# A residual added by VectorE in PSUM instead of by GpSimd, and another order of a scan layer's work on four engines

## The reference

```
h = x @ fc1_w.T + fc1_b
xz = h @ in_proj_w.T;  xc, z = split(xz)
u = silu(conv4(xc) + conv_b)                     # 512 channels
dt_low, Bm, Cm = split(u @ x_proj_w.T)           # 16, 16, 16
dt = softplus(dt_low @ dt_proj_w.T + dt_proj_b)
h[t] = exp(dt[t] * A) * h[t-1] + dt[t] * u[t] * Bm[t];   y[t] = sum_n h[t] * Cm[t]   # 16 states
s = ((y + u * D) * silu(z)) @ out_proj_w.T @ fc2_w.T + fc2_b
g = (silu(xn @ wg.T) * (xn @ wu.T)) @ wd.T       # 768 hidden
out = x + s * silu(g)
```

## Time and profile before

| | us |
|---|---|
| median of 3 runs (3019.51 to 3027.25) | 3020.09 |
| the profiled execution | 3014.55 |
| its span | 3012.9 |
| the scan layer in it, from its first instruction | about 1010 to 3013 |

### The profile page before, as it was taken

The page is one execution under the profiler, slowest core; times in us unless marked ns, Lnnn a source line. Parts: engine busy times, 40 slices in busy tenths (PEclk is TensorE's granted clock), DMA queues, the critical chain, the costliest instruction groups (busy, mean ns, idle before and its releaser), DMA issues.

```text
span 3012.9 us, 43961 instructions
## 1 busy us (share of the span) xinstructions
PE 2588.0 (86%) x13290; PEld 1488.0 (49%) x13290; DVE 2306.4 (77%) x2777; ACT 2027.6 (67%) x3268; POOL 2069.9 (69%) x650
## 2 busy tenths in 40 slices
PE   6776188888887769998999899999899899999987
PEld 2333033333333435564665555656556566566455
DVE  6577466556562269989889799898798888989995
ACT  3221146656564379878788698797787887978874
POOL 0454430000000179999999899999899999999996
PEclk9998579989998879999999999999999999999999
DMA  8335497767641123032132130321312303213210
GB/s 274 105 103 127 109 266 210 186 175 180 172 140 46 55 120 120 30 119 100 36 120 85 65 120 33 117 99 36 121 52 97 120 17 126 105 38 120 78 63 7
DMA packets 133934, 323.21 MB, mean 107 GB/s; under 512 B 13233, under 2 KB 89009, under 8 KB 117314
## 3 DMA queue, kind: packets, MB, share of 16 engines
q1 hardware_dynamic: 113186, 248.84, 26.7%
q0 software_dynamic: 19200, 70.73, 7.1%
q10 hardware_dynamic: 1312, 0.66, 0.1%
HBM read 277.12 MB, written 43.13 MB: 106 GB/s over the span
## 4 chain that ended last, share of the span: by engine, by line
PE 26%; issue 12%; POOL 12%; ACT 7%; DVE 7%; ACTq 1%; DVEq 1%; DMA 0%; POOLq 0%; SPq 0%
PE l_p_w L1995 11%; PE l_p_y L1987 6%; POOL l_st L1638 5%; PE l_p_w L2041 5%; DVE l_st L1457 4%; POOL l_st L1630 3%; PE l_p_w L2060 3%; ACT l_p_a L1716 2%; POOL keep_xg L1638 2%; DVE keep_xg L1457 1%; ACT L1791 1%; POOL l_dtu L1644 1%; ACT L1725 1%; DVE keep_xg L1466 1%; PE l_p_w L2017 1%
## 5 line engine op out<-in xcount | busy, mean ns | idle before, releaser
L1457 DVE TENSOR_TENSOR_SCAN l_st<-l_p_a,l_hl,l_st 128x512 f32<-128x512 f32 x768 | 931.6, 1265 | 112.1 <-ACT l_p_a L1716 93.0
L1638 POOL TENSOR_TENSOR l_st<-l_st,l_cs 128x2048 f32<-128x2048 f32 x192 | 868.6, 4541 | 4.1 <-ACT l_hl L1721 3.8
L1716 ACT ACTIVATE l_p_a<-l_dt,lw_a_neg 128x512 f32<-128x512 f32 x1024 | 666.1, 681 | 51.6 <-DVE keep_xg L1457 40.4
L1630 POOL TENSOR_TENSOR l_st<-l_bs,l_dtu 128x2048 f32<-128x2048 f32 x128 | 580.9, 4539 | 47.5 <-PE l_p_y L1987 44.2
L1987 PEld LDWEIGHTS l_p_y<-keep_ident,l_st 128*128 128x128 f32 x3072 | 353.8, 144 | 136.9 <-POOL l_st L1638 74.8
L1987 PE MATMUL l_p_y<-keep_ident,l_st 128*128 128x128 f32 x3072 | 382.4, 281 | 42.9 <-POOL l_st L1638 42.9
L977 ACT ACTIVATE a_pr<-a_p_s 128x512 f32<-128x512 f32 x512 | 284.8, 596 | 163.9 <-PE a_p_s L1043 145.7
L901 DVE TENSOR_REDUCE a_mpart<-a_p_m 128x1 f32<-128x512 f32 x512 | 315.2, 683 | 98.2 <-PE a_p_m L1008 96.5
L1457 DVE TENSOR_TENSOR_SCAN keep_xg<-l_p_a,l_hl,keep_xg 128x512 f32<-128x512 f32 x256 | 314.8, 1267 | 2.3 <-DVE keep_xg L1466 1.9
L1638 POOL TENSOR_TENSOR keep_xg<-keep_xg,l_cs 128x2048 f32<-128x2048 f32 x64 | 290.7, 4542 | 11.0 <-ACT l_hl L1721 11.0
L1043 PE MATMUL a_p_s<-a_qst,kx 99*128 99x256 bf16 x1024 | 206.7, 292 | 73.6 <-ACT a_pr L977 54.8
(11 more groups left out here) (225 smaller groups left out, 3920.1 us busy)
## 6 DMA issues: line engine op xcount, KB each, us to landing
a_w<-in_w_dram POOLq DMA_DIRECT2D x64, 1024.0 KB, 12.0
l_bs<-s_bc SPq DMA_DIRECT2D x64, 1024.0 KB, 4.7
l_cs<-s_bc SPq DMA_DIRECT2D x64, 1024.0 KB, 4.9
keep_share<-s_x SPq DMA_DIRECT2D x32, 512.0 KB, 4.4
s_kp<-t_kp SPq DMA_DIRECT2D x96, 128.0 KB
kx<-s_kp SPq DMA_DIRECT2D x16, 768.0 KB, 11.8
s_vp<-t_vo SPq DMA_DIRECT2D x16, 544.0 KB
a_vg<-s_vp SPq DMA_DIRECT2D x16, 544.0 KB, 11.7
```

The costliest lines, as they stand in the source:

```text
L1457: eng.tensor_tensor_scan(st[k % NG][:, n, :], p_a[:, n, :], st[k % NG][:, n, :], hl[:, k, n:n + 1], ALU.mult, ALU.add).then_inc(scan_ok, 1)
L1630: eng.tensor_tensor(st[n][:, :, :], bs[:, 4 * n:4 * n + 4, :], dtu[(k // NG) % 2][:, :].unsqueeze(1).broadcast_to([P, NG, TT]), ALU.mult). ...
L1638: eng.tensor_tensor(st[n][:, :, :], st[n][:, :, :], cs[:, 4 * n:4 * n + 4, :], ALU.mult).then_inc(cm_ok, 1)
L1716: eng.activation(p_a[:, n, :], dt[c % 2][:, :], ACT.Exp, scale=a_neg[:, c, m:m + 1]).then_inc(dA_ok, 1)
```

## The change

`mixed` now does all of a tile's end: the product with the gate is written back into PSUM (`mixed_out`), and a third VectorE instruction adds `xt` and writes `gate`. GpSimd's `residual` and its semaphore `res_ok` are gone, and SyncE waits for the second half of `op` instead. Beside this the calls in `period` of all four engines stand in another order, and so does `FILLS`. The shape and number of the other operations are the same; GpSimd's stream only moves its period's start (weighed 11 and 12 now open the next period), does weighed(0) before step_input(1), and does the norm's small product earlier. The start of a tile's own exp rows, and gate_h(4), gate_h(5), gate_z(3), have moved over the border of the period, so that they are called for tile f.

```diff
-        FILLS = (("up", 4, END, 1), ("dt", 1, SCAN, 0), ("up", 5, END, 1), ("tr", 0, FRONT, 1), ("dn", 0, END, 0),
+        FILLS = (("yb", 2, END, 0), ("g", 4, END, 0), ("up", 4, END, 1), ("g", 5, END, 0), ("z", 3, END, 1),
...
@@ sync
-                        eng.wait_ge(res_ok, f + 1)
+                        taken(eng, "op", f, 1)
...
@@ vector, mixed
-                    eng.wait_ge(ob_ok, t * 2 + h + 1)
+                    eng.wait_ge(ob_ok, t * 4 + 2 * h + 1)
                     taken(eng, "dn", t, h)
-                    eng.tensor_tensor(gate[:, 2 * h:2 * h + 2, :], mixed_out, gate[:, 2 * h:2 * h + 2, :], ALU.mult)\
+                    eng.tensor_tensor(mixed_out, mixed_out, gate[:, 2 * h:2 * h + 2, :], ALU.mult).then_inc(ob_ok, 1)
+                    eng.wait_ge(ob_ok, t * 4 + 2 * h + 2)
+                    eng.wait_ge(old_in, t * 16 + 16)
+                    eng.tensor_tensor(gate[:, 2 * h:2 * h + 2, :], mixed_out, xt[:, 2 * h:2 * h + 2, :], ALU.add)\
                        .then_inc(done["op"], 1)
...
@@ gpsimd
-                def residual(t):
-                    taken(eng, "op", t, 1)
-                    eng.wait_ge(old_in, t * 16 + 16)
-                    eng.tensor_tensor(gate[:, :, :], gate[:, :, :], xt[:, :, :], ALU.add).then_inc(res_ok, 1)
...
@@ tensor, period, from up(4) on
                     if end:
+                        back(q, f, p, 2)
+                        sums(f, 12)
+                        gate_h(q, f, p, 4)
+                        sums(f, 13)
                         up_h(q, f, p, 4)
+                        gate_h(q, f, p, 5)
+                        gate_z(q, f, p, 3)
+                        up_h(q, f, p, 5)
...
```

More of the change, by code:

```diff
@@ L1511, in period @@
                         dbu(s, 0)
-                    if end:
-                        hidden(f, 3)
-                    if scan:
                         scan_unit(s, 0, 0)
+                        scan_unit(s, 0, 1)
                     if end:
@@ L1594, in period @@
                         scan_unit(s, 11, 3)
+                        gated(s, o, 1)
                         dbu(s, 12)
-                        hidden(s, 1)
+                    if nxt:
+                        norm_aggr(q + 1)
+                    if scan:
                         scan_unit(s, 12, 0)
@@ L1657, in period @@
                     if end:
+                        weighed(f, 11)
+                        weighed(f, 12)
                         dbu(f, 15)
@@ L1678, in period @@
                         step_input(s, o, 2)
-                    if end:
-                        residual(f)
-                    if scan:
                         weighed(s, 4)
@@ L1806, in period @@
                     if scan:
+                        exp_unit(s, 0, 0)
+                        exp_unit(s, 0, 1)
+                        exp_unit(s, 0, 2)
+                    if end:
+                        gate_h(f, 4)
+                    if scan:
+                        exp_tables()
                         exp_unit(s, 0, 3)
-                    if front:
-                        normed(q)
-                    if scan:
                         exp_unit(s, 1, 0)
@@ L2075, in period @@
                     if end:
+                        sums(f, 14)
+                        sums(f, 15)
                         down(q, f, 0)
+                        down(q, f, 1)
                     if front:
@@ L2079, in period @@
                     if end:
-                        sums(f, 15)
-                    if front:
-                        conv_in(q, q, p, 0)
-                        conv_in(q, q, p, 1)
-                    if end:
-                        down(q, f, 1)
                         back(q, f, p, 3)
@@ L2088, in period @@
                         sums(s, 0)
+                        gate_z(q, s, o, 0)
+                        gate_z(q, s, o, 1)
+                    if front:
+                        conv_in(q, q, p, 0)
+                    if scan:
+                        sums(s, 1)
+                        step_low(q, s, 2)
                     if end:
@@ L2111, in period @@
                         back(q, s, o, 0)
-                    if front:
-                        conv_in(q, q, p, 3)
-                    if scan:
-                        sums(s, 5)
-                        step_low(q, s, 3)
-                        sums(s, 6)
+                        up_h(q, s, o, 0)
+                        sums(s, 7)
+                        gate_h(q, s, o, 1)
+                        sums(s, 8)
+                        gate_h(q, s, o, 2)
+                        back(q, s, o, 1)
                     if front:
```

320 lines of the change are left out of this document (148 added, 172 removed).

## The result

The changed kernel takes 3056.75 us (median of 4 runs, 3056.18 to 3058.35), the kernel before 3023.67 beside it (3019.51 to 3027.87). The ratio is 1.011, with a 95% interval of 1.0091 to 1.0129: it is slower, by about 33 us. The forecast was 3049 with a range of 2998 to 3074. The profiled execution of the changed kernel took 3056.6 (span 3054.7), against 3014.55 before.

A forecast was written before the change was run, and what follows sets the result against it. The period was taken as GpSimd's own work plus waits for TensorE. Terms +35.4 (loop), +6.4 (outside), -10 (back edges), -3 (start) made +28.8 on 3014.55, 3043.4; with 5.5 to the median, 3049 us, range 2998 to 3074.

The forecast's parts named there:

- the two stretches: Weighed(15) to dbu(5), then dbu(5) to dbu(7): GpSimd would wait 5.0 us and 2.9 us for TensorE.
- the twelve periods: Loop periods without back-edge cost: each 121.0 us against 118.05, +2.95, adding +35.4 us over twelve.
- TensorE's three gaps: New TensorE waits before back(3), xc(0) and g(0): 0.45, 0.55 and 0.9 us per period in the loop.
- No other on GpSimd inside a period: GpSimd would wait inside a period only at dbu(5) and dbu(7), about 5 and 2.9 us, both released by TensorE.
- Outside the loop: Periods 14 and 15 would take 120.25 us each, +3.2 twice, +6.4 in all.
- the 0.55 of z(0): In the loop xc(0) waits 0.55 us for z(0)'s gate to load its table and read the bank.
- X: Stretch from weighed(15) to dbu(5): 24.2 us of TensorE's path in the loop, about 21.5 in period 16.
- The back edges: Loop jumps, now between up(3) and back(2): 2 us less per edge, -10 in all, bounds 0 and -29.
- Start and end: Period 1's weighed(0) no longer behind step_input(1): -3 us, bounds 0 and -4.5; the very end: 0.
- the clock rival: TensorE's clock drops between weighed(15) and dbu(7) each period: +27 us on top, 3076; chance 0.10.
- Edges hidden: Stops at the loop's jumps wholly hidden, waits at their floor: -16 us, 3004; chance 0.12.
- GpSimd's cut is the gain: GpSimd is the bound; waits stay 2.62, each of fifteen removed residuals saves 2.33 us: -35, 2985; chance 0.12.

## Why the prediction was right, and where not

**The waits.** Right in sign, place and size. The forecast for the two stretches was 5.0 and 2.9, measured 4.96 and 2.94; the period 121.0, measured 121.03; the twelve periods +35.4, measured +35.8. That they agree to a few hundredths is in part luck: TensorE's three gaps came to 1.50 and not 1.90, and the rest of its way through both stretches to about 0.7 more than I had added up. Leaving out 2.6 inside the first stretch shortened the period by 2.6, leaving out 1.7 inside the second by 1.0 to 1.7, and the same 1.7 outside them by nothing. The gaps were 0.34, 0.44 and 0.72 (forecast 0.45, 0.55, 0.9).

**"No other on GpSimd inside a period"** was wrong. Two of the four waits are put on GpSimd by ScalarE. It changed no number: the run with last(2) and last(4) early turned them into TensorE's.

**Outside the loop** I let the 0.55 of z(0) fall away, because the table would be loaded ahead. It did not. ScalarE itself was busy until 2810.0, so the load began when it does in the loop, and xc(0) waited 0.47:

```profile
2810.06 1.28 ACT L1778 ACT_TABLE_LOAD   x1
2811.35 1.27 ACT L1778 ACTIVATE l_sz<-l_p_w,lw_b_in 128x512 f32<-128x512 f32 x2
```

```profile
2812.18 1.96 PE L1985 MATMUL l_p_w<-l_xnT,lw_w_in 128*128 128x512 f32 x4 [0.47 <-ACT l_sz L1778]
```

The first period came to +3.8, not +3.2. The second is +4.7. I had said that without front blocks X would be 21.5, 2.3 of waiting; measured were 2.12 at weighed(2) and 1.87 at dbu(5), 4.0. Some of the +4.7 is the kernel before's: its period 15 to 16 took 115.02 in one profile and 116.75 in another with the same code there.

**The back edges** are the step where the path was wrong. I took 2 off each, -10, as TensorE had blocks from the jump to sums(15) to cover its stop. But GpSimd meets TensorE earlier, at dbu(1), which waits for sums(13). Ahead of that stand only back(2), sums(12) and g(4) behind the jump, and dbu(1) waits 1.71 to 3.81. The rest are waits for ScalarE's last(k), above all last(2), longer than in an undisturbed period. So each edge still costs 5.2 to 5.6. How long TensorE stands says little about that: where it stood 3.25 and not 4.48, its last block before the jump, up(3), had started later (76.7 after dbu(5), against 74.9), and it resumed at nearly the same time (81.9 and 81.4).

How much the edges gave back is not settled to better than some us. The two profiled executions say 3.3, the medians say more. By medians the loop costs the kernel before about 44 and the changed one 28.6. A part of that has nothing to do with the jumps, as the loop's periods are longer than the written-out ones even without one: by the profiles 1445.72 - 12 x 117.03 - 30.4 = 11 in the kernel before, and 3 in the changed one. That leaves about 33 against 26, so 7 were given back. The kernel before differs from edge to edge: its five periods with one took 122.85, 124.43, 121.40, 127.73 and 124.29, and its runs lie over 23 us (3008.7 to 3031.7). The changed one's took 126.60, 126.43, 126.25, 126.55 and 126.45, and its four runs lie within 2.2 us.

**The total** owes something to luck. For the profiled execution the sum was 3043.4 and 3056.6 was measured, 13 more. I then added 5.5, because the kernel before had been profiled that much below its median; the changed kernel's profiled execution is at its median (3056.6 and 3056.75), so this term was no property of it, and it brought the miss down to 8.

**Start and end.** -2.0 for -3, and +1.1 for 0.

The rivals: the granted clock in the stretches stayed at 1.00, so nothing of the clock rival came. Edges hidden is refuted by the 28.6 that writing the loop out gives back. That GpSimd's cut is the gain is refuted twice for the loop: alone it leaves the period of the old order at 118.04, and 3.09 put back in the new one cost 0.1. The rule of the Trainium skill (Perfetto Trace Analysis, section Identifying the Most-Contended Engine), that the engine of highest occupancy is the bottleneck, named GpSimd; this case's traces do not agree, since in the loop its 2.33 came back as 2.14 + 0.15 of waiting.

I was also wrong about the kernel before, though no term rested on it: I had priced GpSimd's cut at 35 if its one wait stayed. In the old order it stayed, and a second came at dbu(9).

## What to carry to other kernels

When two engines hand each other work in a ring, follow both from one meeting point to every later one before pricing a cut. A stretch in which the busiest engine waits for nothing can hide a partner that would have been ready only 0.04 us earlier (2.33 cut, 2.14 + 0.15 of waiting). Add up per stretch what each engine has between the same two meetings: the larger sum is the time, and a block has a price only in the stretch where its engine is the later one. A block that is put off is late for its reader, and for all that stands behind the reader on its engine. And ask of every stop which meeting comes first behind it: slack that ends at a later meeting covers nothing at the first.

## What was not expected of the hardware

A loop of six turns over all engines cost 44 us of 3020 in one kernel and 28.6 of 3057 in the other, of which the five jumps have about 33 and 26. The rest is that the loop's periods are longer even without a jump. In them table loads wait with their block that outside it run ahead, and dependent instructions of VectorE's `mixed` start 0.84 apart where outside it is 0.73; no run takes these two apart. The five jumps stop TensorE for 3.1 to 5.1 us each, its next matmuls run at the lower clock, and in one execution one edge cost 3.35 us and the next 9.68 over an undisturbed period. Twelve periods of straight code showed no such stop in either kernel. The Trainium skill (Advanced Engine Details and Errata, section Control Flow Timing) gives a branch about 51 ns and a compare-and-branch about 108 ns; the shortest stop at a jump here, 3.1 us, is over 28 times the larger of the two, so something else than the branch itself is in it, and no run here shows what. One hint is on the pages of the profile: the DMA queues marked "instruction" moved 2.97 MB in the kernel before and 2.46 in it written out, 2.92 and 2.47 in the changed one. So with the jumps more was moved there, not less; that the engines stand for it is not shown.
